# Moving a unit's query and key projection, first norm and splits to earlier steps, and its stack loads to a later one, in a two-layer AdaLN kernel

## What is computed

```python
mod = (silu(c) @ wmod).reshape(32, 6, 1, -1)            # sa, ca, ga, sb, cb, gb
h = layernorm(x) * (1 + ca) + sa
x = x + ga * attention(h)                                # 16 heads of 8 numbers, softmax over 256 keys
h = layernorm(x) * (1 + cb) + sb
x = x + gb * experts(h)                                  # 16 experts, top 2 of them for every row
```

## Time and profile before

| what | value |
|---|---|
| time, median of three runs | 1710.71 us (1701.66 to 1714.39) |
| the profiled execution's own time | 1714.06 us |
| its span | 1712.0 us |
| busy: TensorE, VectorE, ScalarE, GpSimd | 1357.1, 1295.8, 1090.8, 1012.4 us |
| mean granted clock of TensorE | 0.929 |
| memory traffic over the span | 164 GB/s |

### The profile page before, as it was taken

One profiled execution on the slowest core, in us unless ns is written; L12 is line 12 of the kernel. 1 busy time (PEld: TensorE's weight loads), 2 busy tenths in 40 slices (PEclk: granted clock), 3 DMA queues, 4 the chain that ended last, 5 costly groups with the idle time before them and its releaser, 6 DMA issues.

```text
span 1712.0 us, 45414 instructions
## 1 busy us (share of the span) xinstructions
PE 1357.1 (79%) x14409; PEld 836.8 (49%) x14409; DVE 1295.8 (76%) x3854; ACT 1090.8 (64%) x2558; POOL 1012.4 (59%) x1416
## 2 busy tenths in 40 slices
PE   2788887888888888888999889888989778875541
PEld 1244444455555445555555555555556445554431
DVE  5678898878887887779988898789878756743422
ACT  1388786767776767677777667676767655642321
POOL 1223335733674777477866777477856881686573
PEclk9999999999998989899999999999999988987765
DMA  4766665566766766766667766676657856556763
GB/s 104 173 150 154 153 155 142 150 144 166 178 171 157 173 174 182 178 161 164 183 175 171 176 155 166 171 173 166 184 159 193 211 160 137 163 165 172 212 191 101
DMA packets 447672, 283.04 MB, mean 165 GB/s; under 512 B 33772, under 2 KB 436750, under 8 KB 447438
## 3 DMA queue, kind: packets, MB, share of 16 engines
q1 hardware_dynamic: 412334, 237.12, 55.4%
q0 software_dynamic: 16384, 33.59, 7.0%
q10 hardware_dynamic: 18720, 9.44, 1.9%
HBM read 171.75 MB, written 108.18 MB: 164 GB/s over the span
## 4 chain that ended last, share of the span: by engine, by line
POOL 25%; PE 23%; DVE 18%; issue 16%; DMA 8%; SPq 6%; ACT 2%; POOLq 0%; ACTq 0%; DVEq 0%
DVE mx L1657 8%; POOL slot_dram L696 8%; POOL y_in L717 5%; PE ps_job L1109 5%; PE ps_s L1243 3%; DMA h_blk<-slot_dram 3%; DMA max_dram<-mx_t 2%; POOL ln_rs L662 2%; PE ps_q L1082 2%; POOL qk_part L743 2%; POOL qk_rest L739 2%; PE ps_q L1065 2%; SPq L525 1%; PE ps_q L1097 1%; POOL x L729 1%
## 5 line engine op out<-in xcount | busy, mean ns | idle before, releaser
L1657 DVE TENSOR_REDUCE mx<-ps_s 128x2 f32<-128x512 f32 x1024 | 655.9, 683 | 106.2 <-PE ps_s L1243 104.3
L894 ACT ACTIVATE prob<-ps_st 128x512 f32<-128x512 f32 x1024 | 558.0, 595 | 94.9 <-PE ps_st L1249 92.1
L1243 PE MATMUL ps_s<-k_stk,q_stk 51*128 51x256 bf16 x2048 | 361.5, 281 | 129.0 <-DVE mx L1657 72.2
L1249 PE MATMUL ps_st<-q_stk,k_stk 53*128 53x256 bf16 x2048 | 356.1, 280 | 5.8 <-ACT prob L894 5.5
L1109 PE MATMUL ps_job<-prob,v_ext 128*32 128x256 f32 x4096 | 292.3, 405 | 27.5 <-issue 10.3
L1243 PEld LDWEIGHTS ps_s<-k_stk,q_stk 51*128 51x128 bf16 x2048 | 140.5, 95 | 327.1 <-DVE mx L1657 204.3
L696 POOL DMA_INDIRECT slot_dram<-h_row,slot x256 | 256.3, 1001 | 71.0 <-issue 65.5
L717 POOL DMA_INDIRECT y_in<-y_dram,slot x224 | 222.9, 995 | 78.4 <-issue 49.9
L836 ACT ACTIVATE o_sb<-ps_job 128x256 f32<-128x256 f32 x256 | 97.4, 381 | 172.8 <-PE ps_job L1109 167.7
L1109 PEld LDWEIGHTS ps_job<-prob,v_ext 128*32 128x32 f32 x4096 | 116.9, 113 | 132.6 <-issue 36.7
L739 POOL TENSOR_TENSOR qk_rest<-qk_f,qk_part 128x512 f32<-128x512 f32 x64 | 74.5, 1164 | 164.7 <-ACT qk_part L927 164.3
(11 more groups left out here) (206 smaller groups left out, 2649.3 us busy)
## 6 DMA issues: line engine op xcount, KB each, us to landing
w_q<-in_we SPq DMA_DIRECT2D x376, 128.0 KB
h_blk<-slot_dram SPq DMA_DIRECT2D x50, 512.0 KB, 5.7
part_dram<-qk_part SPq DMA_DIRECT2D x128, 192.0 KB
q_stk<-part_dram SPq DMA_DIRECT2D x128, 192.0 KB
k_stk<-part_dram SPq DMA_DIRECT2D x128, 192.0 KB
y_dram<-y_sb SPq DMA_DIRECT2D x46, 512.0 KB, 3.2
part_dram<-qk_part SPq DMA_DIRECT2D x128, 128.0 KB
mod_in<-row_dram SPq DMA_DIRECT2D x64, 192.0 KB
```

The costliest lines, as they stand in the source:

```text
L894: sc.activation(prob[:, (k ^ 1) % 8, :], ps_st[k % 2][:], ACT.Exp).then_inc(exp_done, 1)
L1243: mm = pe.matmul(ps_s[j % 2][:, t * S:(t + 1) * S], q_stk[us.tri][r0:r0 + R_BIAS, hp, t * P:(t + 1) * P], k_stk[us.tri][r0:r0 + R_BIAS, hp ...
L1249: mm = pe.matmul(ps_st[k % 2][:, t * S:(t + 1) * S], k_stk[ut.tri][r1:r1 + R_MAX, hp, t * P:(t + 1) * P], q_stk[ut.tri][r1:r1 + R_MAX, hp, ...
L1657: dve.tensor_reduce(mx[:, hp // 4, :, 4 * par + hp % 4], ps_s[j % 2][:].rearrange("p (t s) -> p t s", s=S), AX_X, ALU.max).then_inc(max_do ...
```

## The change

Offsets move, and the order within a step stays as it was:

- The statistics of the first norm go from offset -43 to -42, `rstd` from -42 to -41, `xn` from -33 to -38, the transposition `h_t` from -27 to -35 (place 5 to place 13), the projection from -23 to -29 (place 9 to place 3).
- The splits go six steps earlier: -22, -21, -19, -18 become -28, -27, -25, -24. `part_rows` goes from -17 to -23 (place 15 to place 9), `stack_rows` from -12 to -7 (place 4 to place 9).
- `h_t` has four buffers in place of three. The semaphore that the transpositions of `h_t` and of the attention's result shared is split into `h_mm` and `ctx_mm`, as the two no longer stand in one step.
- The pieces of experts start four steps earlier in groups 0 to 3 and two steps later in group 4 (146 and 152 in place of 150), and two steps later in group 5 (-104 in place of -106).
- The sum of expert rows comes 14 in place of 13 steps behind the first gather of its unit in groups 0 to 4.

The diff, without the renamed buffers and semaphores of the remaining places:

```diff
         SCATTER[last + 92 + n * 3 // 2 if late < 2 else END + (31, 90)[late - 2] + n] = (UNIT_AT[g] + n // 4, n % 4)
     for i in range(PIECES[g]):
-        QUAD[last + 150 + 64 * (i // 3) + (0, 22, 42)[i % 3] if late < 0 else
-             END + (-106 + 16 * i, -8 + 12 * i, 56 + 8 * i, 112 + 8 * i)[late]] = PIECE_AT[g] + i
+        QUAD[last + (146, 152)[g >= SECOND] + 64 * (i // 3) + (0, 22, 42)[i % 3] if late < 0 else
+             END + (-104 + 16 * i, -8 + 12 * i, 56 + 8 * i, 112 + 8 * i)[late]] = PIECE_AT[g] + i
     for i in range(SIZES[g]):
         first = last + 286 + 8 * i if late < 0 else END + (-2 + 5 * i, 58 + 4 * i, 107 + 4 * i, 152 + 4 * i)[late]
-        apart, lag = (2, 13) if late < 0 else (1, 9)
+        apart, lag = (2, 14) if late < 0 else (1, 9)
         for j in range(2 * TT):
             GATHER[first + apart * j] = (UNIT_AT[g] + i, j)
...
 JOBS = {0: [("av0", 32, 0)], 1: [("sh1", 81, 0)], 2: [("o_t1", 50, 0)], 4: [("av1", 36, 0)],
-        5: [("h_t", -27, 0), ("ctx_t", 53, S)], 6: [("max_t1", 22, 0), ("h2_t", 70, S)],
-        7: [("rank", 87, 0), ("owner", 103, P), ("sh_dn", 87, S)], 8: [("av2", 40, 0)], 9: [("qk", -23, 0)],
+        3: [("qk", -29, 0)], 5: [("ctx_t", 53, S)], 6: [("max_t1", 22, 0), ("h2_t", 70, S)],
+        7: [("rank", 87, 0), ("owner", 103, P), ("sh_dn", 87, S)], 8: [("av2", 40, 0)],
         10: [("wo", 58, 0), ("router", 74, S)], 11: [("sh0", 75, 0)], 12: [("av3", 44, 0)],
-        14: [("max_t0", 14, 0), ("v", 14, S)], 15: [("o_t0", 47, 0)]}
+        13: [("h_t", -35, 0)], 14: [("max_t0", 14, 0), ("v", 14, S)], 15: [("o_t0", 47, 0)]}
 AT = {name: after for jobs in JOBS.values() for name, after, _ in jobs}
...
         xn = sb("xn", [P, TT, D])
-        h_t = [sb(f"h_t{i}", [P, S]) for i in range(3)]
+        h_t = [sb(f"h_t{i}", [P, S]) for i in range(4)]
         qk_f = sb("qk_f", [P, 2 * S])
...
 
             for step in range(FIRST, STEPS):
-                u = at(step, -17)
+                u = at(step, -23)
                 if u:
                     part_rows(u)
-                u = at(step, -12)
+                u = at(step, -7)
                 if u:
                     stack_rows(u)
...
             for step in range(FIRST, STEPS):
-                for i, after in ((0, -42), (1, 63)):
+                for i, after in ((0, -41), (1, 63)):
                     u = at(step, after)
...
                     pool.tensor_tensor(act[0], th_sb[0], u_sb[:], ALU.mult).then_inc(act0_ok, 1)
-                u = at(step, -21)
+                u = at(step, -27)
                 if u:
                     pool.tensor_tensor(qk_rest[:], qk_f[:], qk_part[:, 0, :], ALU.subtract).then_inc(qk_r, 1)
-                u = at(step, -18)
+                u = at(step, -24)
                 if u:
...
 
-                sc.wait_ge(h_ctx_mm, h_turn(u))
+                sc.wait_ge(h_mm, u.no + 1)
                 if u.no == B:
                     sc.wait_ge(mod_ok, 4)
-                if u.has(3):
-                    sc.wait_ge(mxt0_v_mm, u.no - 2)
-                sc.activation(h_t[u.tri][:], ps_job[BANK["h_t"]][:, 0:S], ACT.Identity,
+                if u.has(4):
+                    sc.wait_ge(mxt0_v_mm, u.no - 3)
+                sc.activation(h_t[u.no % 4][:], ps_job[BANK["h_t"]][:, 0:S], ACT.Identity,
                               scale=mod[u.layer][:, 1, u.batch:u.batch + 1],
...
                         take_y(q, half)
-                u = at(step, -33)
+                u = at(step, -38)
                 if u:
...
                     take_qk(u)
-                u = at(step, -22)
+                u = at(step, -28)
                 if u:
                     sc.activation(qk_part[:, 0, :], qk_f[:], ACT.Copy).then_inc(qk_hi, 1)
-                u = at(step, -19)
+                u = at(step, -25)
                 if u:
...
                 if "h_t" in units:
-                    mm = transpose_h(units["h_t"])
+                    transpose_h(units["h_t"]).then_inc(h_mm, 1)
                 if "ctx_t" in units:
-                    mm = transpose_ctx(units["ctx_t"])
-                if "h_t" in units or "ctx_t" in units:
-                    mm.then_inc(h_ctx_mm, 1)
+                    transpose_ctx(units["ctx_t"]).then_inc(ctx_mm, 1)
                 if "qk" in units:
...
                     owners(u)
-                u = at(step, -43)
+                u = at(step, -42)
                 if u:
```

## The result

| kernel | median | range | runs |
|---|---|---|---|
| before | 1712.55 us | 1701.66 to 1714.57 | 4 |
| after | 2041.54 us | 2033.95 to 2047.57 | 4 |

The ratio is 1.194 (95% interval 1.190 to 1.197). The direction was as forecast, but the loss is 329 us in place of the 174 that I predicted, and outside my range.

A forecast was written before the change was run, and what follows sets the result against it. The loop of heads was taken to set the pace, with TensorE waiting most for VectorE's row maxima (204.3 us). Late stack loads added 174 us to 1714, giving 1888, or 1885 on the median's scale; range 1787 to 1981.

The forecast's parts named there:

- my sum: Late stack loads lengthen units 1 to 55, by 2.5 to 4.4 us each depending on stage: together 174 us.
- The path from place 8: Last split, six stores, stack loads, next head's first maxima: 13.8 us from place 8, 14.3 with experts, against 9.41 of work.
- The term for GpSimd's other work in the way: With experts, scatters and gathers often stand ahead of the split in GpSimd's list: half a scatter, 0.5 us, added.
- I keep today's halves: First eight heads of each unit: jobs joining and leaving about cancel, so times stay, within 0.5 us either way.
- a rival, at 0.15: TensorE's stops also lower its clock: 1.2 us times 55 units, 66 us on top, 1951 us; chance 0.15.
- SP's other work behind a new wait: Loads, place 10's maxima and expert weights queue on SP behind the wait for the split; the head is hurt first.
- The moved jobs: Pair 4 could fall from 2.77 to about 1.9 us, but that gain is worth nothing while loads are awaited.
- The removed wait: SP's 199.1 us wait at L521 goes away but gains nothing, as the loads could not start earlier.
- The range: 1787 us with earlier split, faster stores and shorter halves; 1981 with the clock and half the store and landing upper bounds.

The follow-up runs named there:

- stacks_first: The changed kernel with the stack loads issued ahead of the next unit's stores of parts in the step that holds both: 1784.61 us, 1.042 of before.
- act_early_late: The changed kernel, late stacks left in, with the shared expert's activation in layer 1 at offsets 75 and 81 in place of 77 and 83: 1995.81 us, 1.166.
- act_early: The changed kernel with stack loads issued before the stores of parts, and layer 1's shared expert activation at offsets 75 and 81: 1699.32 us, 0.994.

## Why the prediction was right and wrong

Of the 159 us by which the span's growth (333) exceeds my sum (174), the first halves of units 5 to 55 make 72, the path behind place 8 makes 53 and the start, up to unit 5, 31; units 56 on make the rest.

**The path from place 8: right in its links, some too short.** I had 13.8 us without experts; the trace has 14.1. The split was to end at 2.7 us and ended at 2.5, the stores took 3.4 against 3.5, the loads 7.6 from the first issue to the landing against 6.9. With experts I had 14.3, and measured 15.5: (424.00 - 176.37) / 16, with the sum over the first halves of that stage,

```profile
sum 176.37, PE 171.67 PEld 100.01 DVE 143.67 ACT 126.57 POOL 59.59; mean PE 10.73 PEld 6.25 DVE 8.98 ACT 7.91 POOL 3.72
```

The term for GpSimd's other work in the way, half a scatter or 0.5 us, was too small by about 1 us: the split ended 3.95 us behind place 8 in the mean of units 17 to 32, against 2.53 in units 5 to 11. This mechanism is shown: undoing the order alone gave back 257 us.

**"I keep today's halves": wrong in two ways.** This is the step that failed. The first halves were the half of the sum that I took over unchanged, with a bound of 0.5 us.

- Without experts they went from 7.97 to 10.1 us, by the clock. I had the mechanism as a rival, at 0.15, with 1.2 us from the one first half in the earlier trace rows. It belonged in the sum: TensorE stopped for the stacks 55 times, for 4.5 us in the mean. The two kernels with work in the stop show it. The Trainium skill (TensorE: Matmul & The Clock Gate, Part 1) says that TensorE falls to 1.2 GHz when it has been idle; the trace agrees, with 0.50 granted in pair 0 behind the stop in each of units 5 to 11.
- In units 33 to 47 they went from 12.0 to 217.59 / 15 = 14.5 us, by two causes together, the shared expert's bank and the stop. The sums over these first halves in the changed kernel, in stacks_first and in act_early_late:

```profile
sum 217.59, PE 193.54 PEld 117.40 DVE 153.20 ACT 138.21 POOL 84.94; mean PE 12.90 PEld 7.83 DVE 10.21 ACT 9.21 POOL 5.66
...
sum 204.25, PE 176.57 PEld 108.67 DVE 152.87 ACT 135.79 POOL 111.74; mean PE 11.77 PEld 7.24 DVE 10.19 ACT 9.05 POOL 7.45
...
sum 196.84, PE 187.70 PEld 112.89 DVE 151.01 ACT 135.45 POOL 89.19; mean PE 12.51 PEld 7.53 DVE 10.07 ACT 9.03 POOL 5.95
```

With the bank alone in the way they take 13.6 us, with the stop alone 13.1, with neither (act_early) 11.7. I had costed the projection in pair 1 by TensorE's idle time there, 0.8 us, and never asked which bank it writes and who frees it. `free_bank` makes a small job wait until the last job of its bank has been taken. Before the change the next job in the bank stood four places behind the shared expert's second half (`h_t`, at place 5), now the projection stands two behind it. This is the step that I left out, and it was no rival either. Over all of layer 1 and both halves, the bank is worth 85 us with early stacks and 46 with late ones.
- In units 17 to 32 they did stay (176.37 / 16 = 11.0 us against 11.3), by luck: without the stop they take 9.9, so a gain that I had not counted and the lower clock about cancel.

**The start: missed.** `stack_rows` of unit 0 at step -7 falls behind SP's setup at step -10. I named SP's other work behind a new wait, but not the queue that the call was moved past. The first maxima came at 68.3 us in place of 49.3, and my sum had nothing for it.

**The moved jobs: misplaced. The removed wait: nearly right.** The gain was to lie in pair 4, where the path hides it, and the first half was to stay. In stacks_first pair 4 of units 5 to 11 fell from 2.77 to 2.48 us in the mean, not to 1.9, and the units stayed at 17.3. Where units got shorter, 17 to 32, it was in the first half. The wait of 199.1 us at L521 was to be worth nothing. With the loads moved by themselves the kernel took 0.5% less.

**The range.** Its upper end took the clock in full but only half of the other bounds, and had no term for a bank.

## What to carry to other kernels

On a queue that works in order, a call's place in the step matters as much as its step: a load that needs nothing new must not stand behind a store that waits for a late engine. When a job moves, list three things for its new place: what stands ahead of it on its queue, which buffer or bank it takes over and who frees it, and what its own successor is. If the forecast is a stop of TensorE in every round, the lower clock behind it belongs in the sum and not among the rivals.

## What I had not expected of the hardware

Extra multiplications that nobody reads made a stage shorter: with 80 of them per unit in a stop, TensorE was busy 142.00 in place of 125.69 us and the stage took 159.07 in place of 169.53 us, as the granted clock rose from 0.82 to 0.95. It held only for units 5 to 11: in units 12 to 16 the stage got 4 us longer. And the kernel before had medians of 1707 to 1712 us in three sets of runs and 1828 us in the last, on another chip, without a change in it.
